# Global attentions: score banks by head, a fourth bank for the row-maximum pieces, and the weighting between the scores of heads 2 and 3

## The reference

```python
# block 0: 16 query heads, 4 key/value heads, head width 16, causal
att = einsum('bsgmd,btgd->bgmst', q, k) / sqrt(16)
att = softmax(where(causal, -inf, att), axis=-1)
ctx = einsum('bgmst,btgd->bsgmd', att, v);  out = ctx @ wo.T
# block 1: 16 heads of width 16 with rotary positions, keys and values from a latent
scores = einsum('bqhd,bkhd->bhqk', q, k) / sqrt(16)
scores = where(page(key) <= page(query), scores, min);  softmax; out = (attn @ v) @ wo
```

## Time and profile before

| | |
|---|---|
| median of 3 runs | 5195.83 us (5181.3 to 5202.37) |
| the profiled execution | 5158.03 us, span 5156.5 us |
| mean granted clock of PE | 0.887 of full |
| busy, us (share) | PE 4120.5 (80%), PEld 2739.7 (53%), DVE 3024.9 (59%), ACT 2489.3 (48%), POOL 1363.3 (26%) |
| stage B_, 180 to 1010 us | PE 790, DVE 664, ACT 613, POOL 233; clock 0.95 |
| stage G_, 2290 to 3171 us | PE 831, DVE 671, ACT 618, POOL 143; clock 0.89 |

### The profile page before, as it was taken

One profiled execution on the slowest core, in us unless ns is written; L12 is line 12 of the kernel. 1 busy time (PEld: TensorE's weight loads), 2 busy tenths in 40 slices (PEclk: granted clock), 3 DMA queues, 4 the chain that ended last, 5 costly groups with the idle time before them and its releaser, 6 DMA issues. The chain is left out here.

```text
span 5156.5 us, 83448 instructions
## 1 busy us (share of the span) xinstructions
PE 4120.5 (80%) x25572; PEld 2739.7 (53%) x25572; DVE 3024.9 (59%) x5338; ACT 2489.3 (48%) x4335; POOL 1363.3 (26%) x2120
## 2 busy tenths in 40 slices
PE   4799999753999994659999996576996967699687
PEld 2444444343999992324444442454665755466465
DVE  1788878441444543748878783575563447656454
ACT  1377767612545541217767675233553423355343
POOL 1232323124000005011111111133882003388300
PEclk9699989976999997858979898798998989899898
DMA  7322322123121203361422221334451023444211
GB/s 227 40 33 33 51 35 33 45 101 108 49 88 49 70 31 119 123 115 26 64 43 45 43 45 64 109 120 142 155 156 51 28 57 115 147 148 156 73 37 37
DMA packets 327112, 413.90 MB, mean 80 GB/s; under 512 B 40772, under 2 KB 236225, under 8 KB 323196
## 3 DMA queue, kind: packets, MB, share of 16 engines
q1 hardware_dynamic: 278620, 257.43, 15.8%
q0 software_dynamic: 43552, 148.12, 13.5%
q10 hardware_dynamic: 4608, 4.20, 0.2%
HBM read 252.57 MB, written 156.19 MB: 79 GB/s over the span
## 5 line engine op out<-in xcount | busy, mean ns | idle before, releaser
L600 DVE TENSOR_REDUCE G_mpart<-G_pm 128x1 f32<-128x512 f32 (+3 forms) x1024 | 618.4, 651 | 209.6 <-PE G_pm L489 202.2
L600 DVE TENSOR_REDUCE B_mpart<-B_pm 128x1 f32<-128x512 f32 (+3 forms) x1024 | 618.1, 651 | 157.3 <-PE B_pm L489 149.3
L579 ACT ACTIVATE G_p<-G_psc 128x1024 f32<-128x1024 f32 (+1 forms) x576 | 532.9, 977 | 151.7 <-PE G_psc L526 149.9
L579 ACT ACTIVATE B_p<-B_psc 128x1024 f32<-128x1024 f32 (+1 forms) x576 | 532.2, 977 | 134.6 <-PE B_psc L526 132.8
L489 PE MATMUL G_pm<-G_ks,G_qs 48*128 48x512 f32 (+3 forms) x1664 | 466.3, 425 | 100.3 <-DMA G_ks<-G_one 58.4
L489 PE MATMUL B_pm<-B_ks,B_qs 48*128 48x512 f32 (+3 forms) x1664 | 453.7, 410 | 74.8 <-DMA B_ks<-B_one 42.5
L489 PEld LDWEIGHTS G_pm<-G_ks,G_qs 48*128 48x128 f32 x1664 | 253.0, 212 | 421.3 <-DVE G_mpart L600 210.7
L1786 POOL TENSOR_SCALAR J_pr<-J_pr,J_rc 128x256 f32<-128x256 f32 x512 | 462.8, 916 | 39.9 <-DVE J_rc L1924 37.5
L489 PEld LDWEIGHTS B_pm<-B_ks,B_qs 48*128 48x128 f32 x1664 | 241.8, 200 | 386.2 <-DVE B_mpart L600 218.7
L504 PE MATMUL G_po<-G_p,G_v 128*32 128x512 f32 (+3 forms) x2560 | 326.6, 592 | 0.1
L526 PE MATMUL G_psc<-G_qs,G_ks 50*128 50x512 f32 (+3 forms) x1280 | 307.0, 418 | 9.3 <-issue 6.8
(11 more groups left out here) (303 smaller groups left out, 7895.3 us busy)
## 6 DMA issues: line engine op xcount, KB each, us to landing
J_v<-lve SPq DMA_DIRECT2D x64, 520.0 KB, 3.8
J_k<-lkT SPq DMA_DIRECT2D x64, 512.0 KB, 4.9
lve<-I_v SPq DMA_DIRECT2D x64, 260.0 KB, 2.1
lqT<-I_tT SPq DMA_DIRECT2D x64, 256.0 KB, 2.4
lkT<-I_tT SPq DMA_DIRECT2D x64, 256.0 KB, 2.6
J_q<-lqT SPq DMA_DIRECT2D x64, 256.0 KB, 3.8
ein<-Z_z SPq DMA_DIRECT2D x8, 1228.0 KB
E_xin<-ein POOLq DMA_DIRECT2D x8, 1152.0 KB, 6.2
```

The costliest lines, as they stand in the source:

```text
L579: act.activation(p[:, t % PSLOTS, 2 * pr:2 * pr + 2, span(t)], psc[:, 2 * pr:2 * pr + 2, span(t)], ACT.Exp, scale=SC).then_inc(e_done[pr], 1)
L600: dve.tensor_reduce(mpart[:, heads[0] % 2, a:z, qb, kc], pm[slots[e]][:, 0:len(heads) * w].rearrange("p (h k) -> p h k", k=w), AX, ALU.max ...
```

## The change

- `psc` becomes three separate banks. Score number `4t + h` goes to bank `(4t + h) % 3`, so a score waits for the exponential three scores before it (`e_done`, now one semaphore counted by head).
- `RING` becomes 4: four `pm` banks.
- ACT takes one exponential for each head, 512 columns, four in a step.
- PE's step becomes: scores of heads 0 and 1, event 0, score of head 2, W, score of head 3, then events from 1 on. In a step with two narrow blocks, both blocks of a head follow one another.
- POOL's clears and PE's weighting wait on the counted semaphore.

```diff
-    RING = 3
+    RING, SBANKS = 4, 3
...
-        psc = ctx.enter_context(nc.psum_tensor(tag + "psc", [P, GRP, CH], F32))
+        psc = [ctx.enter_context(nc.psum_tensor(f"{tag}psc{i}", [P, CH], F32)) for i in range(SBANKS)]
...
-                    wait_apart(pool, e_done[pr], i * NS + t + 1, fence)
+                    wait_apart(pool, e_done, i * (NS * GRP) + t * GRP + 2 * pr + 2, fence)
...
-                for pr in range(2):
-                    pe.wait_ge(e_done[pr], i * NS + t + 2)
+                pe.wait_ge(e_done, i * (NS * GRP) + t * GRP + GRP + 1)
...
-                    for pr in range(2):
-                        pe.wait_ge(e_done[pr], i * NS + t + 1)
+                    def score(h):
+                        if not static(i, 0) or t * GRP + h >= SBANKS:
+                            pe.wait_ge(e_done, i * (NS * GRP) + t * GRP + h + 2 - SBANKS)
                         for kb, off, at in parts:
-                            for h in (2 * pr, 2 * pr + 1):
-                                rows = slice(64 * (h % 2), 64 * (h % 2) + R + 2)
-                                score = pe.matmul(psc[:, h, at:at + CH - off],
-                                                  ks[s][rows, h // 2 % NA, kb * P:(kb + 1) * P],
-                                                  qs[s][rows, qc, h // 2, off:CH], start=True, stop=True)
-                        score.then_inc(s_done, 1)
-                        some(pr, pr + 1)
-                    if t >= 2:
-                        weigh(i, s, t - 2)
-                    elif not static(i, 0):
-                        weigh(i - 1, 1 - s, NS - 2 + t)
-                    some(2, NE)
+                            rows = slice(64 * (h % 2), 64 * (h % 2) + R + 2)
+                            last = pe.matmul(psc[(t * GRP + h) % SBANKS][:, at:at + CH - off],
+                                             ks[s][rows, h // 2 % NA, kb * P:(kb + 1) * P],
+                                             qs[s][rows, qc, h // 2, off:CH], start=True, stop=True)
+                        last.then_inc(s_done, 1)
...
+                    score(0)
+                    score(1)
+                    some(0, 1)
+                    score(2)
+                    weigh_behind()
+                    score(3)
+                    some(1, NE)
...
-                    for pr in range(2):
-                        act.wait_ge(s_done, (i * NS + t) * 2 + pr + 2)
+                    for h in range(GRP):
+                        act.wait_ge(s_done, i * (NS * GRP) + t * GRP + h + 2)
...
-                        act.activation(p[:, t % PSLOTS, 2 * pr:2 * pr + 2, span(t)],
-                                       psc[:, 2 * pr:2 * pr + 2, span(t)],
-                                       ACT.Exp, scale=SC).then_inc(e_done[pr], 1)
+                        act.activation(p[:, t % PSLOTS, h, span(t)], psc[(t * GRP + h) % SBANKS][:, span(t)],
+                                       ACT.Exp, scale=SC).then_inc(e_done, 1)
```

More of the change, by code:

```diff
@@ L298, in attention @@
         s_done, pv_done = sem(tag + "s_done"), sem(tag + "pv_done")
-        e_done = [sem(f"{tag}e_done{i}") for i in range(2)]
+        e_done = sem(tag + "e_done")
         cleared = sem(tag + "cleared")
@@ L519, in some, with weigh_behind @@
                             event(i + nxt, e, (s + nxt) % 2)
-                    for pr in range(2):
-                        pe.wait_ge(e_done[pr], i * NS + t + 1)
+                    def score(h):
+                        if not static(i, 0) or t * GRP + h >= SBANKS:
+                            pe.wait_ge(e_done, i * (NS * GRP) + t * GRP + h + 2 - SBANKS)
                         for kb, off, at in parts:
-                            for h in (2 * pr, 2 * pr + 1):
-                                rows = slice(64 * (h % 2), 64 * (h % 2) + R + 2)
-                                score = pe.matmul(psc[:, h, at:at + CH - off],
-                                                  ks[s][rows, h // 2 % NA, kb * P:(kb + 1) * P],
-                                                  qs[s][rows, qc, h // 2, off:CH], start=True, stop=True)
-                        score.then_inc(s_done, 1)
-                        some(pr, pr + 1)
-                    if t >= 2:
-                        weigh(i, s, t - 2)
-                    elif not static(i, 0):
-                        weigh(i - 1, 1 - s, NS - 2 + t)
-                    some(2, NE)
+                            rows = slice(64 * (h % 2), 64 * (h % 2) + R + 2)
[3 more added lines that the diff above has]
+                        last.then_inc(s_done, 1)
+                    def weigh_behind():
+                        if t >= 2:
+                            weigh(i, s, t - 2)
+                        elif not static(i, 0):
+                            weigh(i - 1, 1 - s, NS - 2 + t)
+                    score(0)
[5 more added lines that the diff above has]
+                    some(1, NE)
             pe.wait_ge(c_in, 16 * CONSTS)
```

## The result

The changed kernel takes 5316.12 us (median of 4 runs, 5302.78 to 5379.07) beside 5191.39 for the kernel before (4 runs, 5181.3 to 5202.37): a ratio of 1.0275, 95% interval 1.0219 to 1.033. It is **slower by 125 us**; the forecast was 5169, its range ended at 5240. The profiled execution took 5302.78 us, span 5300.9, mean granted clock 0.862 (0.887 before). In the changed kernel L525 is the scores, L503 W, L586 the exponentials, L606 the maxima of the pieces.

A forecast was written before the change was run, and what follows sets the result against it. The ring of three pm banks, not a busy engine, was taken to bound the step at 2.70 us. B_ at -16.5 and G_ at -10.5 sum to -27 us, so 5196 becomes 5169; range 5100 to 5240.

The forecast's parts named there:

- The loop of 2.62 us: In each full-width step, score, exponential, next score and W form a closed loop through three score banks: 2.62 us.
- The tails: Last 18 steps of each attention, without pieces: from 2.04 to 2.62 us a step, +9.5 us in each attention.
- Exponentials by head: ACT's four exponentials of 512 columns a step, 0.52 each: +56 us of busy time an attention, still below the stage.
- The steady gain: Whole iterations of both attentions: from 99.57 to 96.1 us, a gain of 3.5 an iteration.
- +5.2 heavy windows: Steps where DVE or ACT work outlasts the loop: 5.2 us an iteration, with ends of 1 and 8.
- floor of 90.9: An iteration of 36 steps at 2.62 us, less 0.85 for each of four narrow steps: at least 90.9 us.
- POOL's cover: POOL's clears, covered by the two steps between exponential and weighting: moved by less than 0.3 us, nothing priced.
- The V load: G_'s waits for the next iteration's V: 1.2 us given back in four to six iterations, 6 us.
- The clock: No term of its own in the sum; a fall to the lower clock only in the tail, as rival C.
- rival C: The clock falls in the tail: at least 3.5, some 3.7 us a step, +40 us, 5209; chance 0.10.
- Rival A: The ring was everything: DVE's bubble goes, DVE bounds at about 91 us an iteration, -100 us, 5096; chance 0.22.
- Rival B: Head 2's score stands behind a piece waiting for DVE: loop 2.80 us a step, 5261 or 5235; chance 0.18.

The follow-up runs named there:

- e1: The changed kernel with four score banks and three piece banks in place of three and four: 5425.2 us, ratio 1.044.
- e3: The kernel before with one exponential for each head in place of one for each pair, nothing else: 5194.93 us, ratio 1.0012.
- e4: The changed kernel with the next iteration's loads issued at step 2 in place of step 4: 5319.47 us, ratio 1.0254.
- e2: The changed kernel with three piece banks in place of four, still three score banks: 5529.8 us, ratio 1.0673.
- e7: The changed kernel with four score banks, three piece banks and event 1 put back ahead of W: 5378.8 us, ratio 1.0339.
- e5: The changed kernel with the scores of heads 0 and 1 computed twice in each step: 5261.66 us, ratio 1.0121.
- e14: The kernel before with three groups of four W-shaped matmuls (128 rows) ahead of G_'s wait for V: 5157.52 us, ratio 0.9954.
- e9: The changed kernel with 20 extra piece-shaped matmuls (48 rows) ahead of G_'s wait for V: 5342.66 us, ratio 1.0389.
- e10: The kernel before with 12 extra piece-shaped matmuls (48 rows) ahead of G_'s wait for V: 5194.4 us, ratio 1.0022.
- e6: The kernel before with the next iteration's loads issued at step 2 in place of step 4: 5271.45 us, ratio 1.0133.
- e13: The changed kernel with five groups of four W-shaped matmuls (128 rows) ahead of G_'s wait for V: 5292.69 us, ratio 1.0225.

## Why the prediction was wrong, point by point

- **The loop of 2.62 us: right.** The tail of the kernel after, PE's and ACT's timelines:

```profile
999.74 1.06 PE L503 MATMUL B_po<-B_p,B_v 128*32 128x512 f32 x8
...
1001.92 0.49 PE L525 MATMUL B_psc<-B_qs,B_ks 50*128 50x512 f32 x1 [0.45 <-ACT B_p L586]
1002.34 1.06 PE L503 MATMUL B_po<-B_p,B_v 128*32 128x512 f32 x8
```

```profile
1001.27 2.06 ACT L586 ACTIVATE B_p<-B_psc 128x512 f32<-128x512 f32 x4 [0.54 <-PE B_psc L525]
```

  W to W 2.60; score (1000.73) to exponential 0.54, exponential 0.60, 0.05 to the score, 0.42 to W, 0.99 of W: each link within 0.01 of its row before. Banks of four dissolve it (e1).
- **The tails: right.** The last iteration of G_, where the clock held, went from 80.4 to 90.4 us, +10.0 for +9.5; B_'s, with 13.7 us at the lower clock, to 95.5.
- **Exponentials by head: right.** ACT's exponentials of B_ went from 532.2 to 589.6 us of busy time, +57 for +56, and e3 is level. Four start 0.49 apart ((2.06 - 0.60) / 3), not 0.52.
- **The steady gain: wrong size.** "+5.2 heavy windows" on the floor of 90.9 should have given 96.1; the sum of shortest steps is 97.60, so they cost 6.7, between the 5.2 that I took and the 8 of my upper end. The other 0.6 of the miss is the start: the sum of shortest steps before is 98.98, and I had subtracted from one whole iteration of 99.57. The gain is 1.4 an iteration, not 3.5: -20 for both attentions, not -52.
- **POOL's cover: gone, which I had named and priced at nothing.** In most of the six middle iterations of B_ the clears behind POOL's 13 issues come too late for W. Timelines of POOL and PE, kernel after:

```profile
865.20 1.18 POOL L345 DMA_DIRECT2D B_v<-vs  x1
866.39 1.84 POOL L356 TENSOR_SCALAR_AFFINE_SELECT B_p<-B_p 128x256 f32<-128x256 f32 x5
```

```profile
867.93 1.07 PE L503 MATMUL B_po<-B_p,B_v 128*32 128x384 f32 x16 [1.25 <-POOL B_p L356]
```

  W waits for POOL 7.2 us in B_ and 3.2 in G_, against 1.1 and none: +9. With it the undisturbed iteration shows no gain at all (99.3, 99.5).
- **The V load: right in kind, too small.** PE waited 27.1 us (5 times, longest 5.8) for 11.0, +16 for +6. The time from V's issue to the stand shrank by more than the 1.2 I had shared out to the steps there: V was issued at 2543.42 and PE stood from 2568.26 before, 24.8 us later, and from 2493.25 after an issue at 2470.61 now, 22.6 us. That is 2.2 us a wait, and a landing 0.7 later, at five waits for four.
- **The clock: this is the step that failed.** The terms above sum to -20 + 20 + 9 + 16 = +25, still on the line of what can be told. Low time grew by 464 - 218 = 246 us, at 0.38 each 94. Together 119 of the 129 measured. I had priced every other term at the full clock and kept the lower clock for rival C, in the tails alone. There it hardly came in the profiled execution (13.7 us in one of them); in e4 it came in both, 64.6 us for 18 steps or 3.59 a step, which is the 3.5 to 3.7 that C had priced. In the profiled execution the lower clock came behind the waits for V, 181 of the 246 us, where the row that I quoted for that wait is followed by W at 1.94: I took the one as a price of transfer and the other as a price for the tail, and did not see that they are one event.
- **Rival A** is out: the bubble of DVE did not close (idle ahead of maxima 149.3 to 186.6 us in B_). **Rival B** named the outcome (an iteration that gains nothing; slower), though not by its mechanism: pieces wait less for DVE than before.

Shown by runs: the loop and what breaks it (e1), the worth of the piece bank and the price of the order (e1, e2, e7), that more matmuls in the changed step shorten the low stretches (e5), that the kernel before loses 24 us to its own waits for V (e14), that a lower clock costs 0.38 in this kernel (14 steps, and four executions of the whole). Argued only: that the 0.38 holds in each low stretch, and so the 94 us. **Open**: how much of the longer low stretches is due to the changed step and how much to waits of 5.2 us and more in place of 3.0 and less, and what in the step keeps the clock down. More matmuls of 50 rows in the step shortened the stretches (e5), matmuls of 48 rows in the wait did not (e9). PE's record is full in that stretch (64.48 us busy of 64.50), so its busy share does not tell it; and a profile is one execution, whose low time varies: B_ had 64 to 67 us of it in two kernels with the same B_ as before (the kernel before, e10), 51 in a third (e14).

## What to carry to other kernels

Before pricing a change at the full clock, read where the clock falls now, and how long it stays down: those places multiply whatever the change adds to the wait ahead of them or takes from PE's work behind them. A bank taken from one ring and given to another moves the bound, so close both loops on paper, with the order of issue as it will be, and check the new order with the old banks by itself. When an edit takes a wait away, read the new trace for the waits that it makes (e4, e6) before calling the wait tested. And a wait that nobody can shorten may be worth filling with work of the right shape.

## What the runs showed of the hardware

- The wait for V is followed by low stretches of 6.8 to 17.1 us in two programs (before, e5) and of 20.5 to 71.7 in a third (after), by rows in which PE is busy for nearly all of that time (64.48 of 64.50 us).
- What fills the wait matters, not that it is filled: with 48-row matmuls in it (e9, e10) the clock fell at the waits for V as without them (198 and 65 us low there, against 239 and 58), once with no gap ahead (e9, at 2409.1); with 128-row matmuls in four column strips it did not fall there at all in the kernel before (e14), and for 51 us in the changed one (e13). The Trainium skill (TensorE: Matmul & The Clock Gate, Part 1, HAM oscillation) asks for a PE without long idle gaps. In e9 the gap was 0.30 us, and W behind it took 1.93, so here the absence of a gap was not enough.
- Four matmuls of 512 columns in four column strips take 0.93 us together (2.78 for three such groups, e14), and an exponential of 512 columns 0.60 alone and 0.49 in a row.
- While POOL issues DMAs its record shows nothing else: from the first of the 13 issues to the end of the last 7.8 us pass (2618.83 to 2626.62 in e6), and what waits behind them stalls DVE for up to 6.4 us and PE for up to 6.3 (e6).
